# The start of a fused state-space and expert layer: the first mixer in a new order on all engines, its step size on VectorE

## The reference, cut to what matters

```
z, B, C, dt_raw, X = x @ Wz, x @ Win (split into four)
delta = softplus(dt_raw + dt_bias)                       # step size, 8 heads
h_t = exp(-delta_t * exp(A_log)) * h_(t-1) + X_t * delta_t * B_t;  y_t = h_t C_t + D * X_t
x1 = layernorm(x + (y * (silu(z) @ Wzg)) @ Wout)
dw1, dw2, dw3 = top-3 softmax weights of x1 @ P_w.T @ U.T      # 12 experts each
h = gelu(sum_e dw1[e] * (x1 @ W1[e].T))
out = layernorm(x1 + sum_e dw2[e] * (h @ W2[e].T) + dw3 @ b2)
```

## Time and profile before

| | us |
|---|---|
| median of three runs (1566.17 to 1568.41) | 1566.34 |
| the profiled execution | 1565.38 |
| its span in the profile | 1563.7 |
| PE busy | 1545.0 |
| DVE busy | 1108.0 |
| POOL busy | 663.7 |
| ACT busy | 598.1 |

### The profile page before, as it was taken

The page is one execution under the profiler, slowest core; times in us unless marked ns, Lnnn a source line. Parts: engine busy times, 40 slices in busy tenths (PEclk is TensorE's granted clock), DMA queues, the critical chain, the costliest instruction groups (busy, mean ns, idle before and its releaser), DMA issues.

```text
span 1563.7 us, 25298 instructions
## 1 busy us (share of the span) xinstructions
PE 1545.0 (99%) x8634; PEld 1249.2 (80%) x8634; DVE 1108.0 (71%) x3108; ACT 598.1 (38%) x1362; POOL 663.7 (42%) x755
## 2 busy tenths in 40 slices
PE   8999999999999999999999999999999999999998
PEld 6778788888888878888788888878888788887876
DVE  7577676877768687676776768777686776867755
ACT  6652424425144351533425244242443515335130
POOL 7681623616145270643616336162451715436040
PEclk9999999999999999999999999999999999999999
DMA  5350312304023040321403123040230403214020
GB/s 176 102 158 22 116 41 66 98 29 132 19 76 88 29 135 14 103 69 46 118 17 118 44 66 98 29 128 22 71 93 29 136 14 99 73 40 125 15 74 7
DMA packets 81600, 114.79 MB, mean 73 GB/s; under 512 B 10160, under 2 KB 37312, under 8 KB 81472
## 3 DMA queue, kind: packets, MB, share of 16 engines
q1 hardware_dynamic: 81472, 113.18, 24.9%
HBM read 108.02 MB, written 5.13 MB: 72 GB/s over the span
## 4 chain that ended last, share of the span: by engine, by line
PE 92%; POOL 4%; issue 1%; DVE 1%; DMA 1%; ACT 0%; SPq 0%; POOLq 0%; DVEq 0%; ACTq 0%
PE exp_bank L246 22%; PE exp_bank L248 22%; PE exp_bank L247 22%; PE mix_bank L893 4%; PE mix_bank L919 3%; PE mix_bank L246 3%; PE mix_bank L247 3%; PE mix_bank L248 3%; PE mix_bank L901 3%; PE mix_bank L790 1%; PE turn_bank L1224 1%; POOL w_lo L445 1%; PE mix_bank L738 1%; POOL Wt L853 1%; PE mix_bank L1010 1%
## 5 line engine op out<-in xcount | busy, mean ns | idle before, releaser
L1167 POOL TENSOR_TENSOR sp_lo<-fbuf,sp_hi 128x512 fp32r<-128x512 f32 (+2 forms) x203 | 246.6, 1218 | 179.3 <-ACT sp_hi L1164 112.7
L246 PE MATMUL exp_bank<-w_hi,sp_hi 128*128 128x512 f32 x768 | 307.5, 400 | 0.8 <-POOL sp_lo L1217 0.8
L246 PE MATMUL exp_bank<-sp_hi,w_hi 128*128 128x512 f32 x764 | 304.9, 399 | 2.2 <-POOL sp_lo L1167 2.0
L248 PE MATMUL exp_bank<-w_hi,sp_lo 128*128 128x512 f32 x768 | 303.2, 395 | 0.0
L247 PE MATMUL exp_bank<-w_lo,sp_hi 128*128 128x512 f32 x768 | 303.1, 395 | 0.0
L248 PE MATMUL exp_bank<-sp_hi,w_lo 128*128 128x512 f32 x764 | 300.5, 393 | 0.0
L247 PE MATMUL exp_bank<-sp_lo,w_hi 128*128 128x512 f32 x764 | 298.8, 391 | 0.0
L1264 DVE SCALAR_TENSOR_TENSOR acc<-exp_bank,dw,acc 128x128 f32<-128x128 f32 x384 | 132.2, 344 | 152.9 <-PE exp_bank L248 152.2
L1164 ACT CAST sp_hi<-fbuf 128x512 fp32r<-128x512 f32 (+2 forms) x203 | 120.0, 591 | 277.2 <-DVE fbuf L1134 217.2
L853 POOL TENSOR_TENSOR Wt<-Wt,Gh 128x512 f32<-128x512 f32 x128 | 184.9, 1446 | 23.0 <-DVE Wt L845 22.9
L246 PEld LDWEIGHTS exp_bank<-sp_hi,w_hi 128*128 128x128 f32 x764 | 143.6, 188 | 43.2 <-issue 8.0
(11 more groups left out here) (267 smaller groups left out, 2281.4 us busy)
## 6 DMA issues: line engine op xcount, KB each, us to landing
row_b<-dw_rows SPq DMA_DIRECT2D x190, 256.0 KB, 3.4
seg_b<-dA_rows SPq DMA_DIRECT2D x124, 256.0 KB, 3.6
ctd<-cum_rows SPq DMA_DIRECT2D x128, 96.0 KB, 3.3
x_in<-in_x SPq DMA_DIRECT2D x16, 256.0 KB, 2.8
result<-acc SPq DMA_DIRECT2D x15, 256.0 KB, 2.3
fbuf<-in_W1T SPq DMA_DIRECT2D x12, 256.0 KB, 4.2
acc<-in_W2T SPq DMA_DIRECT2D x5, 256.0 KB, 4.0
x_in<-in_W2T SPq DMA_DIRECT2D x3, 256.0 KB, 4.4
```

Of the source, the lines that this page charges most:

```text
L246: nc.tensor.matmul(ps, s_hi, m_hi, start=start and j == 0, stop=False)
L248: last = nc.tensor.matmul(ps, s_lo, m_hi, start=False, stop=stop and j == n - 1)
L1167: sig("xw_lo", PO.tensor_tensor(lo[:, cols], wide[e % 2][:, cols], hi[:, cols].bitcast(F32), ALU.subtract))
```

## The change

The order of the steps in the start is new on every engine, and with it where some work is done:

- `mix_step` of both batches runs on DVE, reciprocal included. Its second part is a call of its own, so that other steps stand between the parts.
- POOL begins with a wait for the sixth cast of DVE, `skip_tables` and `mix_ends`.
- `Xde` of the first batch lies in `zg` (`Xde0`), which the gate's result fills later; it does not wait for the gate's rests.
- ACT makes all high parts of W1, and copies `unit_bank`. DVE makes the rests of tiles 0 and 1 only.
- On PE the dummy products between the rates and the states, and before the output product, are gone; zg groups stand around the states.
- DVE goes on to x1 when tile 8 is split, and waits for the others before the logits.
- SP sends the first decay row as soon as it is written, and loads weight tiles 4 and 5 behind the decay rows.

The diff, without the hunks that only rename, split a range or add a wait on a semaphore named in the text:

```diff
@@ -135,6 +135,7 @@
         silu = Wt[:, 0, :].rearrange("p (k t) -> p k t", k=NK)
         strict = zg[:, 0, 0:P]
         Xde = Wt[:, :, :].rearrange("p a b -> p (a b)")[:, 0:(NC - 1) * DI].rearrange("p (c n) -> p c n", c=NC - 1)
+        Xde0 = zg[:, :, :].rearrange("p a b -> p (a b)")[:, 0:(NC - 1) * DI].rearrange("p (c n) -> p c n", c=NC - 1)
 
         rows = sb("rows", [P, P])
         row_b = [sb(f"row_b{n}", [P, T]) for n in range(2)]
...
@@ -347,6 +348,8 @@
                 PE.wait_ge(sems["ident"], 2)
             if eng is AC:
                 AC.preload_act_table_set(LOG_EXP)
+                AC.wait_ge(sems["ident"], 2)
+                AC.copy(unit[:, :], ident4[:, :]).then_inc(sems["unit"], 1)
                 AC.wait_ge(sems["pad"], 5)
 
         def setup_z(eng):
...
@@ -431,17 +431,11 @@
             for k in ks:
                 _, hi, lo = w_tile(k)
                 at, landed, n = w_stage(k)
-                if k < NHP:
-                    if eng is DVE:
-                        DVE.wait_ge(landed, n)
-                        DVE.tensor_copy(hi, at).then_inc(sems["w_hi_v"], 1)
-                        DVE.wait_ge(sems["w_hi_v"], k + 1)
-                elif eng is AC:
+                if eng is AC:
                     AC.wait_ge(landed, n)
                     AC.copy(hi, at).then_inc(sems["w_hi"], 1)
                 if eng is (DVE if on_dve(k) else PO):
-                    if k >= NHP:
-                        eng.wait_ge(sems["w_hi"], k - NHP + 1)
+                    eng.wait_ge(sems["w_hi"], k + 1)
                     eng.tensor_tensor(lo, at, hi.bitcast(F32), ALU.subtract).then_inc(sems["w_lo1" if on_dve(k) else "w_lo0"], 1)
 
         def load_b2(eng):
...
@@ -768,11 +770,14 @@
                 sig("end_dt", PO.tensor_tensor(ends[:, :], ends[:, :], flat, ALU.mult))
                 wait(PO, "end_dt", b)
                 alone(PO)
+                if first(b):
+                    PO.wait_ge(sems["cast"], 4)
+                else:
+                    wait(PO, "silu_lo", b)
                 for c in range(NC - 1):
                     wait(PO, "Xd", b, c + 1)
-                    wait(PO, "silu_lo", b)
                     sig("Xde", PO.tensor_tensor(
-                        Xde[:, c, :].rearrange("p (h n) -> p h n", h=H), Xd[:, c, :].rearrange("p (h n) -> p h n", h=H),
+                        (Xde0 if first(b) else Xde)[:, c, :].rearrange("p (h n) -> p h n", h=H), Xd[:, c, :].rearrange("p (h n) -> p h n", h=H),
                         ends[:, c * H:(c + 1) * H].unsqueeze(2).to_broadcast([P, H, HD]), ALU.mult))
 
         def mix_states(eng, b):
...
@@ -839,7 +844,11 @@
                     DVE.wait_ge(sems[f"seg{h % 4}"], 16 * (h // 4 + 1))
                 else:
                     wait(DVE, f"seg_in{h % 2}", b, h // 2 + 1)
-                wait(DVE, "ps_st", b)
+                if first(b):
+                    DVE.wait_ge(sems["unit"], 1)
+                    wait(DVE, "silu_lo", b)
+                else:
+                    wait(DVE, "ps_st", b)
                 if q >= 2:
                     wait(DVE, "ps_yq", b, q - 1)
                 sig("scan", DVE.tensor_tensor_scan(W, first_seg[h % 4] if first(b) else seg_b[h % 2][:, :], unit[:, :], 0.0, ALU.mult, ALU.add))
@@ -1433,32 +1442,32 @@
             mix_bc(PE, b)
             PE.wait_ge(sems["cast"], 3)
             mix_z(PE, b)
-            mix_X(PE, b, range(4))
+            mix_X(PE, b, range(2))
             PE.wait_ge(sems["masks"], 6)
             PE.wait_ge(sems["cast"], 4)
             mix_rates(PE, b)
             mix_ends(PE, b)
+            mix_X(PE, b, range(2, 4))
             router_product(PE)
-            keep_busy(rb, 6)
             mix_scores(PE, b)
-            keep_busy(rb, 12)
-            mix_states(PE, b)
             mix_x(PE, nxt, True)
             PE.wait_ge(sems["router"], 1)
             PE.wait_ge(sems["cast"], NCAST)
-            mix_zg(PE, b)
+            mix_zg(PE, b, range(1))
+            mix_states(PE, b)
+            mix_zg(PE, b, range(1, 3))
             mix_y_skip(PE, b, 0)
             mix_y(PE, b, 0)
             mix_y_skip(PE, b, 1)
+            mix_zg(PE, b, [3])
+            mix_y(PE, b, 1)
             mix_dt(PE, nxt)
-            mix_y(PE, b, 1)
-            mix_bc(PE, nxt)
             mix_y_skip(PE, b, 2)
             mix_y(PE, b, 2)
             mix_z(PE, nxt)
             mix_y_skip(PE, b, 3)
             mix_y(PE, b, 3)
-            keep_busy(rb, 6)
+            mix_bc(PE, nxt)
             mix_out(PE, b)
             mix_X(PE, nxt, range(2))
             keep_busy(rb, 14)
@@ -1481,18 +1490,18 @@
             mix_x(DVE, b)
             setup_z(DVE)
             neg_a_ready(DVE)
+            mix_step(DVE, b, on=DVE, parts=(0,))
             setup_masks(DVE)
-            split_w(DVE, range(0, 2))
-            mix_step(DVE, b)
+            mix_step(DVE, b, on=DVE, parts=(1,))
+            setup_zg(DVE)
             mix_z(DVE, b)
-            mix_X(DVE, b, range(2))
-            mix_silu_split(DVE, b, on=DVE)
+            mix_X(DVE, b, range(3))
             DVE.wait_ge(sems["zero"], 16)
             mix_rates(DVE, b)
-            setup_zg(DVE)
-            mix_X(DVE, b, range(2, 4))
-            split_w(DVE, range(2, 4))
+            mix_silu_split(DVE, b, on=DVE)
+            mix_X(DVE, b, [3])
             router_product(DVE)
+            split_w(DVE, range(2))
             mix_decay(DVE, b, 0)
             mix_decay(DVE, b, 1)
             mix_states(DVE, b)
@@ -1503,13 +1512,16 @@
                 mix_decay(DVE, b, 2 * q + 1)
                 mix_from_start(DVE, b, q)
                 mix_y(DVE, b, q - 1)
-            mix_step(DVE, nxt)
+            mix_step(DVE, nxt, on=DVE, parts=(0,))
             mix_y(DVE, b, NQ - 1)
-            mix_z(DVE, nxt)
+            mix_step(DVE, nxt, on=DVE, parts=(1,))
+            mix_z(DVE, nxt, range(1))
             mix_out(DVE, b)
             route_stats(DVE, b)
+            mix_z(DVE, nxt, range(1, NK))
+            first_weights_ready(DVE, 8)
+            route_scale(DVE, b)
             first_weights_ready(DVE)
-            route_scale(DVE, b)
             route_logits(DVE, b, on=DVE)
             route_weights(DVE, b)
             mix_rates(DVE, nxt)
@@ -1524,41 +1536,46 @@
             setup_zg(AC)
             mix_step(AC, b, table=False)
             mix_z(AC, b)
-            mix_silu_split(AC, b, on=DVE)
             AC.preload_act_table_set(LOG_EXP)
             mix_rates(AC, b)
             mix_ends(AC, b)
+            mix_silu_split(AC, b, on=DVE)
             mix_bc(AC, b)
-            split_w(AC, range(2, 6))
+            split_w(AC, range(2))
             mix_scores(AC, b)
             mix_score_step(AC, b, 0)
             mix_score_step(AC, b, 1)
+            split_w(AC, range(2, 4))
             mix_x(AC, nxt, True)
             mix_zg(AC, b, range(1))
             mix_score_step(AC, b, 2)
             mix_zg(AC, b, range(1, 3))
             mix_score_step(AC, b, 3)
-            split_w(AC, [6])
+            split_w(AC, range(4, 6))
             mix_zg(AC, b, [3])
             mix_score_step(AC, b, 4)
             mix_score_step(AC, b, 5)
+            split_w(AC, [6])
+            mix_score_step(AC, b, 6)
+            mix_score_step(AC, b, 7)
             split_w(AC, [7])
-            mix_score_step(AC, b, 6)
-            split_w(AC, [8])
-            mix_score_step(AC, b, 7)
             mix_dt(AC, nxt)
+            mix_step(AC, nxt, table=False, parts=(0,))
+            split_w(AC, range(8, 11))
+            mix_step(AC, nxt, table=False, parts=(1,))
             mix_bc(AC, nxt)
-            mix_step(AC, nxt, table=False)
-            split_w(AC, range(9, 12))
             mix_z(AC, nxt)
             AC.preload_act_table_set(LOG_EXP)
-            mix_silu_split(AC, nxt)
+            split_w(AC, [11])
+            mix_silu_split(AC, nxt, ks=range(1))
             mix_X(AC, nxt, [0], on=AC)
             route_stats(AC, b, table=False)
+            mix_silu_split(AC, nxt, ks=range(1, NK))
             mix_X(AC, nxt, [1], on=AC)
+            split_w(AC, range(N1, N1 + 2))
+            first_weights_ready(AC, 9)
+            route_transpose(AC, b)
             first_weights_ready(AC)
-            split_w(AC, range(N1, N1 + 2))
-            route_transpose(AC, b)
             mix_scores(AC, nxt)
             mix_rates(AC, nxt)
             mix_ends(AC, nxt)
@@ -1575,17 +1592,13 @@
 
         def start_pool(b, nxt):
 
-            neg_a_ready(PO)
-            mix_step(PO, b)
+            PO.wait_ge(sems["cast"], NCAST)
             skip_tables(PO)
             mix_ends(PO, b)
-            split_w(PO, range(4, 6))
             for q in range(NQ):
                 mix_decay(PO, b, 2 * q)
                 mix_decay(PO, b, 2 * q + 1)
-                if 0 < q < NQ - 1:
-                    split_w(PO, [5 + q])
-            mix_step(PO, nxt)
+                split_w(PO, ([2, 3], [4, 5], [6], [7])[q])
```

(9 more changed lines are left out.)

53 lines of the change are left out of this document (29 added, 24 removed).

## The result

The changed kernel takes 1568.73 us (median of 12 runs, 1566.27 to 1571.06) against 1566.30 us before (12 runs, 1562.41 to 1568.41). The ratio is 1.0022, 95% interval 1.0014 to 1.0030: 3.4 us slower by the ratio (2.2 to 4.7), 2.4 by the medians. The profiled execution has a span of 1565.2 us (1563.7 before).

What follows compares the result with a forecast made beforehand. TensorE, busy 1545.0 of 1563.7 us, bounds the kernel and only the start can move. x1 comes 1.2 us later: 1565.38 + 1.2 = 1566.6, and with 0.96 for the median 1567.5 us, range 1562.0 to 1571.0.

Steps and rivals of the forecast that it cites:

- x1: Normalised tile that TensorE transposes ahead of routing: forecast ready at 59.9 against 58.68, 1.2 us later, carried to the end.
- First step on DVE: First batch's step size, moved from GpSimd to VectorE: ends at 14.4 instead of 17.46, 3.1 us earlier.
- First scan: VectorE's first scan: starts at 24.05 instead of 26.39, 2.3 us earlier, after three GpSimd holds of 0.63 us.
- Third scan: VectorE's third scan: starts at 31.4, 1.1 us earlier, with 1.25 us added for two more GpSimd operations.
- The loads: Loads of weight tiles 4 to 7, sent some ten microseconds later behind the decay rows: claimed to cost nothing.
- Third pair of score products: Heads 4 and 5 on GpSimd: ends at 40.8 instead of 40.63, with one more split of 1.28 us ahead.
- Last gate: VectorE's last gating product, now ahead of the step's second half: ends at 47.75 instead of 49.14.
- Output product: TensorE's output product behind the last gating product: starts at 47.85 instead of 49.19, ends at 51.7.
- Second step: Second step size on VectorE: GpSimd's splits hold it 2.75 us, so the residual add starts at 55.05 instead of 53.07.
- the second rival: Every VectorE-GpSimd meeting costs in full: x1 4.7 us later, median 1571.1; chance 0.29 together with low clock and slow instructions.
- The 24 dummy products that go: TensorE dummies removed from the start: said to have stood before waits, so their removal costs nothing.
- the clock as a rival: TensorE's clock falls before x1's transposes and the router product: +1.7 us, 1569.2; shares a chance of 0.29.

Runs made afterwards that it cites:

- e7: Changed kernel with 33 more dummies, splits of tiles 8 to 11 behind the second step, both gates later, third decay row loaded before tiles 4 and 5: 1563.25 us.
- e11: e7 with GpSimd's splits of tiles 5 and 6 each moved behind the next pair of score products, and 6 dummies fewer: 1562.09 us.
- e1: Changed kernel, but GpSimd waits for the end of the second step before splitting weight tiles 8 to 11: ratio 1.0006 to the kernel before.
- e4: Changed kernel with GpSimd's splits of weight tiles 8, 9 and 10 each done twice: ratio 1.0041 to the kernel before.
- e6: Kernel before with only the 24 dummy products taken out that the change took out: ratio 1.0010 to the kernel before.
- e12: Changed kernel with the 24 dummy products put back at their old places: ratio 1.0011 to the kernel before.
- e5: Changed kernel with 38 more dummy products, all in places where its TensorE waits: ratio 1.0000 to the kernel before.

## Why the prediction was right, and where it was short

The forecast, 1567.5 us and no change that can be told, is 1.2 us under the measured median, inside the range. The loss itself was forecast at 1.2 us and measured at 2.4 by the medians and 3.4 by the ratio, so the walk to x1 was right and about half of the loss was not in it. By the ratio the loss is 0.22%, with an interval that reaches to both sides of the bound of 0.2% taken there, so "slower" is as good a name for it. By its steps:

- First step on DVE, forecast to end at 14.4: 14.15, at a pitch of 0.29 to 0.30 us. Right.
- First scan, forecast 24.05: 23.13. Of three holds of 0.63 one came in part (the running product, 0.80 for 0.4); the two gate rests took 1.25 together, as alone. Another of 1.0 came at the two weight rests (2.27 for 1.2), where none was forecast. POOL was held in turn: three state weights took 4.86 us.
- Third scan, forecast 31.4: 31.76, but 0.92 of it is a wait for the third decay row, whose load stood behind those of tiles 4 and 5. The loads, costed at nothing, cost that; e7 took it away and the scan came at 30.80. That the forecast is met within 0.4 is luck: fewer holds and an unforeseen wait cancel.
- Third pair of score products, forecast to end at 40.8: 41.14. Last gate, forecast to end at 47.75: 48.13. Output product, forecast to start at 47.85: 48.19. Right within 0.4, and e11 shows the cause (a split between the pairs).
- Second step, forecast with one random and two chained holds, 2.75 us, and the add at 55.05: three holds, 2.6 us together (0.89 + 1.14 + 1.13 less 3 x 0.18), and 55.09. e1 and e4 show that POOL's splits are the cause. By the Trainium skill ("SBUF — State Buffer", section "Who interferes with whom") a VectorE instruction with two SBUF inputs, or in a two-port form, contends with GpSimd, and one with a single SBUF input outside those forms does not. The runs agree on both: the TENSOR_TENSOR of 1.29 us in e4, and the RECIPROCAL of 0.35 us there beside a split. The step's first part was held twice as well (1.12, 1.15), which I had not costed; it lay in DVE's wait for the fourth y.
- x1, forecast 59.9: 59.88. As to the time, the order costs 1.7 to 1.9 us in the table above, forecast 1.2. The holds that the forecast adds up are 1.9 + 1.25 + 2.75 = 5.9 us, not the 5.3 named beside the second rival; with the 1.9 us that are then missing to 3.1, that rival decides from 7.8 us and not from 7.5.
- **The step that failed:** "The 24 dummy products that go stood before waits of PE [...]: nothing." They cost 1.6 us in the old order (e6) and, less surely, 1.7 in the new (e12), about the other half of the loss, and the granted clock fell with them in both. Behind it stands a misread row: the nines of PEclk in the earlier trace rows mean 90% or more of full clock in slices of 39 us, not a full clock, and a window of 5 us in the kernel before (60 to 65) has 0.66. I had the clock as a rival with a price of 1.7 us, but only behind x1; it fell there (the router product took 1.77 us for 1.08), and also between 15 and 25 us, behind two waits of 2.51 and 1.01 us with little work between them. The Trainium skill ("TensorE: Matmul & The Clock Gate", section "A second HAM failure mode: psum-queue depth-cycling") describes a neighbouring case, a bf16 kernel in which many very short idle times between groups of products let the clock go down and up, which costs throughput while the typical product stays fast. Here the idle times are fewer and longer, and single products do get slow (1.77 for 1.08 us); that short waits can cost clock, the runs show as well (0.72 and 0.60 against 1.00 when they were filled, in e5).

Of the 2.9 us by which routing ends late in the profiled execution (its rows at 73.43, 70.53 before) the span shows only 1.5. The next router product starts 2.6 us later (141.94, 139.33 before), the last one 1.7 (1471.95, 1470.23); the 0.9 us between are lost by the execution of the kernel before between 902 and 1091 us, and why was not looked into. Single executions of one kernel differ by more than that, so the ratio is what counts.
